# Two chained bottleneck blocks on one Trainium2 core: the last stage with rotating PSUM bank pairs and a written-out order

## The reference, cut to what matters

```
# block 0, with batch norms over the whole batch
out = relu(bn(conv1x1(x, w1) + b1))              # 512 -> 128
out = relu(bn(conv3x3(out, w2) + b2))            # 128 -> 128
out = bn(conv1x1(out, w3) + b3)                  # 128 -> 512
x   = relu(x + softplus(residual_scale) * out)
# block 1, no norms
out = conv1x1(x, w1) + bias1b                    # 512 -> 128
out = conv3x3(out + bias2a, w2) + bias2b         # 128 -> 128
out = conv1x1(out + bias3a, w3) + bias3b         # 128 -> 512
y   = relu(out * rscale + rbias + x)
```

## Time and profile before

| | us |
|---|---|
| median of 3 runs | 327.2 (326.69 to 328.03) |
| the profiled execution, its own time | 325.43 |
| its span, first to last instruction | 323.4 |
| first matmul of the last stage, `conv_a(0, 0)` | 133.24 |
| last matmul, issued | 317.11 |
| mean granted PE clock over the span | 0.962 of full |

### The profile page before, as it was taken

One profiled execution on the slowest core, in us unless ns is written; L12 is line 12 of the kernel. 1 busy time (PEld: TensorE's weight loads), 2 busy tenths in 40 slices (PEclk: granted clock), 3 DMA queues, 4 the chain that ended last, 5 costly groups with the idle time before them and its releaser, 6 DMA issues.

```text
span 323.4 us, 3968 instructions
## 1 busy us (share of the span) xinstructions
PE 285.1 (88%) x1526; PEld 264.8 (82%) x1526; DVE 264.9 (82%) x374; ACT 199.1 (62%) x241; POOL 22.8 (7%) x22
## 2 busy tenths in 40 slices
PE   6789997998999878857768989999999999999972
PEld 3679995988899678636758979999999999999862
DVE  3789988899999748765495988989899897988563
ACT  5698855676563186155383857459588584946463
POOL 0000000000000099800000000000000000000000
PEclk9999999999999979898797999999999999999987
DMA  6999504000000000000000000000403104043168
GB/s 216 424 425 421 213 2 172 0 2 0 0 2 0 0 1 2 0 0 0 2 0 0 0 3 0 0 3 0 199 2 160 41 0 199 2 199 149 52 272 324
DMA packets 5713, 28.17 MB, mean 87 GB/s; under 512 B 832, under 2 KB 2368, under 8 KB 4672
## 3 DMA queue, kind: packets, MB, share of 16 engines
q1 hardware_dynamic: 5408, 27.92, 21.4%
q10 hardware_dynamic: 288, 0.01, 0.1%
HBM read 15.09 MB, written 12.85 MB: 86 GB/s over the span
## 4 chain that ended last, share of the span: by engine, by line
PE 61%; DVE 25%; ACT 6%; issue 4%; DMA 2%; SPq 1%; DVEq 0%; ACTq 0%
PE ps L835 41%; PE ps L870 17%; DVE vl L621 4%; DVE vf L605 3%; DVE stats L644 2%; DMA x<-x_dram 2%; DVE x L739 2%; DVE y L631 2%; DVE vf L609 1%; DVE vf L608 1%; DVE at L698 1%; DVE y L639 1%; DVE xl L538 1%; DVE x L780 1%; DVE a2l L718 1%
## 5 line engine op out<-in xcount | busy, mean ns | idle before, releaser
L446 ACT ACTIVATE x<-x,shift 128x784 f32<-128x784 f32 x32 | 30.3, 948 | 21.4 <-DVE x L739 20.7
L780 DVE SCALAR_TENSOR_TENSOR x<-ps,scal,x 128x784 f32<-128x784 f32 x32 | 32.9, 1029 | 6.3 <-PE ps L835 6.1
L870 PE MATMUL ps<-vh,wu0h 128*128 128x364 f32 (+1 forms) x96 | 33.0, 344 | 4.1 <-DVE vl L621 2.2
L739 DVE SCALAR_TENSOR_TENSOR x<-ps,scale,x 128x784 f32<-128x784 f32 x32 | 32.8, 1027 | 3.6 <-PE ps L835 3.5
L870 PE MATMUL ps<-vl,wu1h 128*128 128x364 f32 (+1 forms) x96 | 32.1, 334 | 0.0
L870 PE MATMUL ps<-vh,wu1h 128*128 128x364 f32 (+1 forms) x96 | 32.0, 333 | 0.0
L870 PE MATMUL ps<-vh,wu0l 128*128 128x364 f32 (+1 forms) x96 | 32.0, 333 | 0.0
L870 PE MATMUL ps<-vh,wu1l 128*128 128x364 f32 (+1 forms) x96 | 31.9, 332 | 0.0
L835 PE MATMUL ps<-a2h,wch 128*128 128x392 f32 x64 | 24.0, 376 | 8.3 <-DVE a2l L718 5.3
L870 PE MATMUL ps<-vl,wu0h 128*128 128x364 f32 (+1 forms) x96 | 31.3, 334 | 0.0
L744 DVE TENSOR_TENSOR xl<-x,xh 128x784 fp32r<-128x784 f32 x32 | 30.6, 963 | 0.8 <-ACT xh L453 0.8
(11 more groups left out here) (156 smaller groups left out, 732.1 us busy)
## 6 DMA issues: line engine op xcount, KB each, us to landing
x<-x_dram SPq DMA_DIRECT2D x15, 784.0 KB, 8.7
out_dram<-x SPq DMA_DIRECT2D x7, 1568.0 KB, 5.2
out_dram<-x SPq DMA_DIRECT2D x4, 392.0 KB, 3.8
raw<-w_dram SPq DMA_DIRECT2D x1, 1088.0 KB, 5.9
x<-x_dram SPq DMA_DIRECT2D x4, 196.0 KB, 4.6
raw<-w_dram SPq DMA_DIRECT2D x1, 576.0 KB, 9.8
...
par<-par_dram ACTq DMA_DIRECT2D x1, 9.0 KB, 3.2
```

The source lines that it names most:

```text
L446: nc.scalar.activation(x_quad(q, c), x_quad(q, c), ACT.Relu, bias=shift3[:, c:c + 1]).then_inc(x1_ready, 1)
L739: nc.vector.scalar_tensor_tensor(x_quad(q, c), ps[:, bank:bank + 2, 0:N], scale3[:, c:c + 1], x_quad(q, c), ALU.mult, ALU.add).then_inc(s_ ...
L780: nc.vector.scalar_tensor_tensor(x_quad(q, c), ps[:, bank:bank + 2, 0:N], scal[:, RSCALE:RSCALE + 1], x_quad(q, c), ALU.mult, ALU.add).the ...
L870: return nc.tensor.matmul(by_row(ps[:, bank, 0:N])[:, :, a:RW - b], wu[part][:, TILE[k] + dw, :], by_row(v[:, k, :])[:, :, b:RW - a], star ...
```

## The change

It touches the last stage only.

1. **Banks.** Four pairs are named SY = 0, SZ = 2, SX = 4, SW = 6. `conv_m`'s k = 0, 1 use SY for odd quads and SX for even ones, k = 2, 3 use SW. From quad 3 on, `conv_a(q)` uses SY for odd q and SX for even q; `conv_b(q)` the same (q = 0: SY). `conv_d` has SZ. At both ends the free pairs are used as well. The waits on banks follow.
2. **Second places.** The split halves of quads 1 and 3 of `conv_a` go to `t2h`, `t2l`, and those of quads 5 and 7 of `conv_d` go to `a2h`, `a2l`.
3. **Start.** The order of all three queues is written out for the first three quads. PE runs a(0), a(1), b(0), a(2), b(1) before `conv_m(0, 0)`, and `conv_b` waits per channel group and no longer on a whole quad's `sum1`. Eight `keep_warm` matmuls stand ahead of `conv_a(0, 3)` (six stood behind `conv_a(0, 1)`). `high_a2(1)` stands behind `square_root`, and `high_a2(2)` ahead of `relu1(0, 0)`; `low_a2(1)` stands ahead of `sum1(0, 0)`.
4. **Loop.** In each round the order inside the DVE and ACT queues is another.
5. **End.** PE runs `conv_m(7)` whole, then `conv_d(6)`, then `conv_d(7)`. Quads 6 and 7 are finished and stored tile by tile, and the last tile in two halves: 7 stores of a tile and 2 of half a tile take the place of one store of a quad and 4 of a tile.

The diff, cut to its core. First the banks and the second places:

```
+        SY, SZ, SX, SW = 0, 2, 4, 6
+        def slot_m(q, k):
+            return (SY if q % 2 else SX) + k if k < 2 else SW + k - 2
         def slot_a(q, c):
-            return 2 * (c % 2) if q < 3 else 0
+            if q < 2:
+                return (SY, SZ, SX, SW)[c]
+            if q == 2:
+                return (SZ, SW)[c % 2]
+            return SY if q % 2 else SX
+        def slot_b(q):
+            return SY if q % 2 or q == 0 else SX
         def slot_d(q, c):
-            return 2 * (c % 2) if q >= Q - 3 else 2
+            return {Q - 4: (SZ, SX, SZ, SX), Q - 3: (SZ, SY, SZ, SX), Q - 2: (SZ, SX, SY, SW), Q - 1: (SZ, SX, SY, SW)}.get(q, (SZ,) * CT)[c]
+        def halves_a(q):
+            return (t2h, t2l) if q in (1, 3) else (a2h, a2l)
+        def halves_t2(q):
+            return (a2h, a2l) if q in (Q - 3, Q - 1) else (t2h, t2l)
```

The stores on SP:

```
+            for q in range(Q - 2):
+                sync.wait_ge(y_ready, 2 * q + 2)
+                sync.dma_start(out[:, 2 * q:2 * q + 2, :, :], x[:, 2 * q:2 * q + 2, :, :]).then_inc(out_stored, 16)
+            for c in range(2 * CT - 1):
+                q = Q - 2 + c // CT
+                sync.wait_ge(y_ready, 2 * (Q - 2) + c + 1)
+                sync.dma_start(out[:, 2 * q:2 * q + 2, c % CT, :], x_quad(q, c % CT)).then_inc(out_stored, 16)
+            for k in range(2):
+                sync.wait_ge(y_ready, 2 * (Q - 2) + 2 * CT + k)
+                sync.dma_start(out[:, U - 2 + k, CT - 1, :], x[:, U - 2 + k, CT - 1, :]).then_inc(out_stored, 16)
+            sync.wait_ge(out_stored, 16 * (Q - 2 + 2 * CT + 1))
```

ACT: the waits of `high_a2` and `high_x`, and the new order:

```
-                if q > 0:
-                    act.wait_ge(a_done, CT * q)
-                nc.scalar.activation(a2h[:, :], y[:, q, :], ACT.Copy).then_inc(a2h_ready, 1)
+                if q == 1:
+                    act.wait_ge(z_ready, 1)
+                    act.wait_ge(m3_done, 1)
+                    act.wait_ge(wcl_ready, 1)
+                if q >= 2:
+                    act.wait_ge(a_done, CT * (q - 1) if q < 5 else CT * q)
+                nc.scalar.activation(halves_a(q)[0][:, :], y[:, q, :], ACT.Copy).then_inc(a2h_ready, 1)
...
-                    act.wait_ge(b_done, q)
+                    act.wait_ge(b_done, CT * (q - 1) + 2 * k + 2)
...
+            high_a2(2)
+            relu1(0, 0)
+            relu1(0, 1)
+            high_x(0, 0)
+            relu1(0, 2)
+            relu1(0, 3)
+            high_x(0, 1)
+            relu1(1, 0)
+            relu1(1, 1)
+            relu1(1, 2)
+            high_x(1, 0)
+            high_a2(3)
+            relu1(1, 3)
+            fill_t1(0)
+            high_x(1, 1)
+            relu1(2, 0)
+            high_v(0, 0)
+            relu1(2, 1)
+            high_v(0, 1)
+            for t in range(Q - 3):
+                high_x(t + 2, 0)
+                if t > 0:
+                    high_t2(t - 1)
+                fill_t1(t + 1)
+                if t == 0:
+                    relu1(2, 2)
+                    relu1(2, 3)
+                high_x(t + 2, 1)
+                if t >= 2:
                     finish(t - 2, 0)
-                if t + 3 < Q:
-                    relu1(t + 3, 2)
-                if 0 <= t - 2 < Q - 1:
+                high_v(t + 1, 0)
+                relu1(t + 3, 0)
+                evacuate_m(t)
+                if t >= 2:
                     finish(t - 2, 1)
-                if t + 3 < Q:
-                    relu1(t + 3, 3)
+                relu1(t + 3, 1)
+                high_v(t + 1, 1)
+                relu1(t + 3, 2)
                 if t + 4 < Q:
                     high_a2(t + 4)
-                if 0 <= t < Q:
-                    high_t2(t)
+                relu1(t + 3, 3)
+            high_t2(Q - 4)
+            finish(Q - 5, 0)
+            high_x(Q - 1, 0)
+            fill_t1(Q - 2)
+            high_x(Q - 1, 1)
+            finish(Q - 5, 1)
+            evacuate_m(Q - 3)
+            high_v(Q - 2, 0)
+            high_t2(Q - 3)
+            finish(Q - 4, 0)
+            high_v(Q - 2, 1)
+            finish(Q - 4, 1)
+            fill_t1(Q - 1)
+            high_v(Q - 1, 0)
+            evacuate_m(Q - 2)
+            high_v(Q - 1, 1)
+            high_t2(Q - 2)
+            finish(Q - 3, 0)
+            evacuate_m(Q - 1)
+            finish(Q - 3, 1)
+            high_t2(Q - 1)
             for c in range(CT):
-                finish_last(c)
+                finish_tile(Q - 2, c)
+            for c in range(CT - 1):
+                finish_tile(Q - 1, c)
+            for k in range(2):
+                finish_half(k)
```

DVE, the new order (of the lines removed none is shown):

```
+            low_a2(1)
+            for c in range(CT):
+                sum1(0, c)
+            sum1(1, 0)
+            sum1(1, 1)
+            low_x(0, 0)
+            low_x(0, 1)
+            low_a2(2)
+            sum1(1, 2)
+            low_x(0, 2)
+            low_x(0, 3)
+            sum1(1, 3)
+            low_x(1, 0)
+            low_x(1, 1)
+            sum1(2, 0)
+            sum1(2, 1)
+            v_sums(0, 0)
+            low_x(1, 2)
+            low_x(1, 3)
+            v_sums(0, 1)
+            v_low(0, 0)
+            low_a2(3)
+            v_low(0, 1)
+            sum1(2, 2)
+            sum1(2, 3)
+            for t in range(Q - 3):
+                low_x(t + 2, 0)
+                low_x(t + 2, 1)
+                if t > 0:
                     low_t2(t - 1)
+                v_sums(t + 1, 0)
+                sum1(t + 3, 0)
+                if t > 0:
                     sum2(t - 1, 0)
+                low_x(t + 2, 2)
+                low_x(t + 2, 3)
+                sum1(t + 3, 1)
+                if t > 0:
                     sum2(t - 1, 1)
+                v_sums(t + 1, 1)
+                v_low(t + 1, 0)
+                sum1(t + 3, 2)
+                if t > 0:
                     sum2(t - 1, 2)
+                t2_sum(t)
+                v_low(t + 1, 1)
+                sum1(t + 3, 3)
                 if t + 4 < Q:
                     low_a2(t + 4)
+                t2_last(t)
+                if t > 0:
+                    sum2(t - 1, 3)
+            low_t2(Q - 4)
+            low_x(Q - 1, 0)
+            low_x(Q - 1, 1)
+            v_sums(Q - 2, 0)
+            sum2(Q - 4, 0)
+            low_x(Q - 1, 2)
+            sum2(Q - 4, 1)
+            low_x(Q - 1, 3)
+            v_low(Q - 2, 0)
+            t2_sum(Q - 3)
+            sum2(Q - 4, 2)
+            t2_last(Q - 3)
+            sum2(Q - 4, 3)
+            v_sums(Q - 2, 1)
+            low_t2(Q - 3)
+            v_low(Q - 2, 1)
+            v_sums(Q - 1, 0)
+            sum2(Q - 3, 0)
+            v_sums(Q - 1, 1)
+            v_low(Q - 1, 0)
+            sum2(Q - 3, 1)
+            t2_sum(Q - 2)
+            v_low(Q - 1, 1)
+            sum2(Q - 3, 2)
+            t2_last(Q - 2)
+            sum2(Q - 3, 3)
+            low_t2(Q - 2)
+            t2_sum(Q - 1)
+            t2_last(Q - 1)
+            sum2(Q - 2, 0)
+            low_t2(Q - 1)
+            for c in range(1, CT):
+                sum2(Q - 2, c)
+            for c in range(CT - 1):
+                sum2(Q - 1, c)
+            for k in range(2):
+                sum2_half(k)
```

PE: `conv_b`, the waits of `conv_m`, and the new order:

```
+            def conv_b(q, c):
+                if q == 0 and c == 0:
+                    pe.wait_ge(wb_ready, 1)
+                    pe.wait_ge(s_ready, CT + 1)
+                if q == 1 and c == 0:
+                    pe.wait_ge(t1_ready, 1)
+                if q > 1 and c == 0:
+                    pe.wait_ge(ta_ready, q - 1)
+                pe.wait_ge(xl_ready, CT * q + c + 1)
+                for k in range(2):
+                    part = slice(k * N, k * N + N)
+                    last = three(slot_b(q) + k, wa1, c, xh[:, c, part], xl[:, c, part], c == 0, c == CT - 1)
                 last.then_inc(b_done, 1)
...
+                if k < 2:
+                    if 0 < q < Q - 2:
+                        pe.wait_ge(s_ready, CT * (q + 3))
+                    elif q > 0:
+                        pe.wait_ge(sum_ready, CT * (Q - 3) if q == Q - 2 else CT * (Q - 3) + 2)
+                elif q == 0:
+                    pe.wait_ge(s_ready, CT * 3)
+                elif k == 2:
+                    pe.wait_ge(tb_ready, q)
+                else:
+                    pe.wait_ge(t2_ready, q)
+                product(slot_m(q, k), wu1, k, vh[q % 2], vl[q % 2]).then_inc(m_done, 1)
...
+            for q in range(3):
                 for c in range(CT):
+                    if q > 0:
+                        conv_a(q, c)
+                if q > 0:
+                    for c in range(CT):
+                        conv_b(q - 1, c)
+            for t in range(Q - 1):
+                for c in range(CT):
+                    conv_m(t, c)
+                    if t + 3 < Q:
                         conv_a(t + 3, c)
+                    if t > 0:
                         conv_d(t - 1, c)
+                if t + 2 < Q:
+                    for c in range(CT):
+                        conv_b(t + 2, c)
+            for k in range(4):
```

(51 more changed lines are left out.)

156 lines of the change are left out of this document (57 added, 99 removed).

## The result

The changed kernel took 308.09 us, the median of four runs (307.26 to 308.67), against 326.94 for the kernel before (326.07 to 328.03). The ratio is 0.942, with a 95% interval of 0.939 to 0.946. In a later set of runs the same kernel had 304.89 us (302.35 to 306.58), ratio 0.933 (0.925 to 0.941) to the kernel before in that set. The forecast was 306.5 us, range 304.0 to 312.0. The profiled execution has a span of 305.5 us where 302.8 was worked out.

A forecast was written before the change was run, and what follows sets the result against it. PE was taken to bound the middle rounds, with time lost at both ends. Gains 14.5 + 1.8 + 5.6 = 21.9 less 1.3 of costs gave span 302.8, plus 2.03 and 1.77 the median 306.5 us, range 304.0 to 312.0.

The forecast's parts named there:

- Start, 14.5 us: Last stage up to conv_m(1, 0): the new order and second places bring it to 179.5 against 194.0, 14.5 us less.
- What the waits of the start cost: Ahead of conv_b(0): PE's idles of 1.1 and 1.4 us and ACT's 2.1 us hold-up were called hidden by DVE's work.
- Rounds, 1.8 us: Rounds 1 to 4: without conv_b's wait on a whole quad's sum1, 19.05 us a round against 19.51, 1.8 us less.
- The tight path to `conv_d(t-1, 0)`: In each round: high_x, two low_x and low_t2 let it start at 2.46, slot at 2.61, 0.15 us to spare.
- Rival 1: Rounds gain nothing or lose, each waiting for low_t2, 19.4 to 20 us; 308.5 to 311 us, chance 0.18.
- End, 5.6 us: From conv_m(5, 0) to the end: conv_d(6) covers quad 7's chain, stores go by tiles; 45.7 against 51.3, 5.6 us less.
- The DMA estimate, 45.4: At the end: nine stores on SP, timed from quad 5's store on, finish 45.4 us behind conv_m(5, 0).
- The two costs, 1.3 us: Set against the gain: slower hand-offs on the start's path, about 0.5, and low clock behind the 2.0 us idle, 0.8.
- Rival 2: Low clock in the start: two to four more spells of 1.5 us behind its idles; 309.5 to 312.5 us, chance 0.10.
- Rival 3: The start fails since ACT holds relu1(0, 0) behind high_a2(2); only rounds and end count; 320.5 us, chance 0.05.
- Rival 4: Slower: changing bank pairs behind short waits, PE falls to the low clock in mid-round; 330.5 us, chance 0.03.
- Its own signs: Trace marks for right or wrong, such as conv_b(0) by 149, conv_m(1, 0) about 180, rounds of 19.1 us without waits.

The follow-up runs named there:

- e3: Changed kernel with quad 1's halves back in a2h, a2l, quad 2 given the second place and high_a2(2) behind high_x(0, 0): 307.71 us.
- e4: Changed kernel with only high_a2(2) moved on ACT, from ahead of relu1(0, 0) to behind high_x(0, 0): 304.15 us.
- e2: Changed kernel with conv_b(2) to conv_b(6) waiting again for all four sum1 of a quad, banks still rotated: 311.21 us.
- e9: Changed kernel with one more DVE instruction, an unread sum over 784 columns, in each of rounds 0 to 3: 307.25 us.
- e5: Changed kernel with PE's old order at the end, conv_m(7, k) and conv_d(6, k) alternating: 311.04 us.
- e6: Changed kernel with quad 6 stored by one DMA when its four tiles are finished, not by four: 307.64 us.
- e1: The changed kernel unedited, run again for a second trace: 304.89 us, ratio 0.933 to the kernel before.

## Why the prediction was right, point by point

**Start, 14.5 us.** Right, and the size nearly. From the stage's first matmul to `conv_m(1, 0)` the forecast had 46.3 us (179.5 - 133.2), the traces of the changed kernel 48.9 and 47.5, the kernel before 60.7. The gain is 11.8 and 13.3 us. The difference is nearly all clock, in two stretches: up to a1 (8.4 forecast, 9.6 and 8.2 measured), and from m0 to m1 (17.2 forecast, 18.4 measured, 17.1 to 17.2 in four traces without the spell). The walk between them, a1 to m0, was 20.7 against 20.95. The runs don't take this gain apart whole: e3 prices the second place, but no run undid the written-out order of the queues or `conv_b`'s wait by channel group alone. For these the evidence is the walk that came true and PE's idle, down by 9.0 us.

**What the waits of the start cost.** This step was wrong. The text said of the 1.1 and 1.4 us ahead of `conv_b(0)` that "what they cost is hidden, since DVE's queue sets the rest", and of ACT's hold-up of `relu1(0, 0)` that it "is hidden behind 38 us of DVE work". e4 shows 1.87 us for it: DVE itself idled for `high_x`, once 1.02 and once 0.75 us. The walk had these idles in its times, so the sum was not hurt; only the reading of it was. DVE is the floor, but the changed kernel stands well above it: 43.1 and 42.7 us from `low_a2(1)` to m1 in its two traces, against 38.1 of steps.

**Rounds, 1.8 us.** Right. Rounds are 19.04 us (19.05 forecast), m1 to m5 76.2 against 78.1 before: 1.9. That "issue" hides the wait on a whole quad's `sum1` is what e2 shows. The tight path to `conv_d(t-1, 0)` held, with no wait in any round. Rival 1 is out, though e9 shows how near it stood.

**End, 5.6 us.** 46.1 measured from m5 to the end against 45.7 forecast and 51.3 before: 5.2. PE never waits, 39.75 us to the last issue where 39.9 were summed, and the last ReLU ends 42.3 us behind m5 where 42.0 were summed. e5 and e6 give the two parts: order 4.2 us, stores by tiles 2.3 (each with the other kept). The DMA estimate, 45.4, and the compute estimate, 45.9, were both within 0.7. The two halves of the last tile took 3.4 us each from issue to landing:

```profile
out_dram<-x SPq DMA_DIRECT2D x2, 196.0 KB, 3.4
```

**The two costs, 1.3 us.** The clock spell came in the first trace at the top of its price (1.25 us against 0 to 1.3, taken 0.8), so DVE hid little of it. Hand-offs were priced at 0.5; the 0.25 us by which a1 to m0 was missed is all that the runs show of them.

**What the sum owes to luck.** The span was missed by 2.7 us, 305.5 for 302.8. The parts: 1.0 ahead of the stage, 1.2 of low clock up to a1, 0.25 in the walk, 1.2 from m0 to m1 and 0.4 at the end, less 0.1 in the rounds and less the 1.3 set aside. The median was missed by 1.6 only, since the other terms were too large: 2.03 + 1.77 us from the span to the median, taken from the kernel before, were 1.76 + 0.83 here. In the set of e1 the span was 303.0, 0.2 from the forecast, and the median 1.6 below it, since there the two terms were 1.75 and 0.14. So both medians lie in the range, but each lies half a per cent from the forecast, one above and one below, by errors that partly cancel.

**Rivals 2, 3, 4.** Rival 2 is out as it was put: of the waits of 1.1, 1.4, 1.0 and 2.0 us only the last has a spell behind it, and the sum had that. The longer low clock at the stage's first matmuls stands ahead of all four. Rival 3 is out. Rival 4 is out: the granted clock is 1.00 from 183.2 to 290, with four bank pairs in turn. The Trainium skill (TensorE: Matmul & The Clock Gate, A second HAM failure mode: psum-queue depth-cycling) puts the swinging clock of its kernel down to PE's short idles between groups of matmuls. The changed kernel has no such idle in its rounds, so it doesn't test that. e2 does so for one idle in a round: it has the same four pairs and 0.49 to 0.51 us of wait in each of the rounds 1 to 4, and its clock is 1.00 too.

**Its own signs.** One of them failed in the first trace. The prediction is wrong, it says, if `conv_b(0)` starts after 149; it started at 149.38 (146.90 in e1). The stage began 1.0 us later and lost 1.2 to the clock, and from a1 on the walk held, so the sign told of the clock and not of the order. DVE was to have no idle over 0.5 us from 156 to 178; it had one of 0.69, waiting for PE behind the spell (0.91 in e1). `conv_m(1, 0)` and `conv_m(5, 0)`, forecast at about 180 and 256, came at 183.2 and 259.4 (180.7 and 256.9 in e1). The other signs hold: rounds of 19.0 us without a wait, no wait of PE at the end, and the end 6.4 us behind the last matmul.

## What to carry to other kernels

Where one engine is full in the middle of a kernel, the time is at the two ends: count the engine's own work between its first and last instruction, and what is left over is what order, buffers and banks can give. Walk the new order in all queues with durations of the old trace; here that gave stretches of 17 to 76 us to within 0.3 wherever the clock was the one assumed. An idle that the walk shows ahead of the bottleneck's steps is a cost until the walk without it has been made too. At the end, stores are a queue of their own: cut what comes last into the pieces in which it gets ready.
